# A pipelined attention stage on one core: the order of the work in a step, masks added by 32-row tiles, and one of eight sums of squares taken by ScalarE

## The reference, cut to what matters

```python
def attn_layer(x, Wqkv, qs, ksc, Wo):
    q, k, v = split(x @ Wqkv)             # 16 heads of 64
    q = l2norm(q) * qs; k = l2norm(k) * ksc
    q = q*cos*scale + rotate_half(q)*sin*scale
    k = k*cos/scale + rotate_half(k)*sin/scale
    # per window of 32 queries and 64 keys
    sim = where(mask, -max, 8.0 * q @ k.T)
    return concat_heads(softmax(sim) @ v) @ Wo
for i in range(6):
    x = attn_layer(shift_tokens(x), ...) + x
    x = ffn_layer(shift_tokens(x), ...) + x     # layernorm, gated gelu, 128 -> 341 -> 128
```

## Time and profile before

| What | Value |
|---|---|
| Median of 3 runs | 2125.77 us |
| Lowest and highest | 2125.34 and 2126.13 us |
| The profiled execution's own time | 2125.36 us |
| Its span, first to last instruction | 2123.6 us |
| Busy: PE, PEld, DVE, ACT, POOL | 1930.0, 1456.1, 1688.3, 1421.5, 1246.3 us |
| Mean granted TensorE clock, as a share of full speed | 0.955 |

### The profile page before, as it was taken

How to read it: one execution, slowest core, us unless ns; L and a number is a source line. 1 busy time by engine, 2 the same in 40 slices (tenths; PEclk the granted TensorE clock), 3 DMA queues, 4 the chain that set the end, 5 groups by cost and what they waited for, 6 DMA issues and landing times. The chain is left out here.

```text
span 2123.6 us, 79458 instructions
## 1 busy us (share of the span) xinstructions
PE 1930.0 (91%) x33524; PEld 1456.1 (69%) x33524; DVE 1688.3 (80%) x3905; ACT 1421.5 (67%) x5112; POOL 1246.3 (59%) x871
## 2 busy tenths in 40 slices
PE   5779999999999999999999999999999995494496
PEld 3358778687786886868868778687686872252374
DVE  5679889698796996978969889698796965795654
ACT  4269779597795985968959779597695972342121
POOL 2268768388584885857858668587584851031000
PEclk9879999999999999999999999999999998696798
DMA  3011122031120211212112121021120110001000
GB/s 114 0 46 42 29 53 57 20 79 34 45 59 22 75 42 36 57 31 72 42 25 63 40 54 54 20 67 48 41 55 18 42 34 13 0 2 61 1 1 21
DMA packets 88229, 85.72 MB, mean 40 GB/s; under 512 B 15392, under 2 KB 83008, under 8 KB 87232
## 3 DMA queue, kind: packets, MB, share of 16 engines
q1 hardware_dynamic: 87872, 80.63, 13.8%
HBM read 25.51 MB, written 1.05 MB: 13 GB/s over the span
## 5 line engine op out<-in xcount | busy, mean ns | idle before, releaser
L1082 POOL TENSOR_TENSOR RN<-N,minus_half 128x8 f32<-128x8 f32 x384 | 632.7, 1648 | 168.8 <-DVE N L1010 168.8
L920 ACT ACTIVATE PB<-PS,NMX 128x64 f32<-128x64 f32 x1536 | 471.4, 337 | 29.9 <-DVE NMX L1030 29.8
L679 PE MATMUL PS<-WQ,XS 128*128 128x256 f32 x1536 | 436.2, 407 | 7.4 <-SPq L623 6.5
L920 ACT ACTIVATION_READ_ACCUMULATOR PB<-PS,NMX 128x1 f32 x1536 | 348.0, 227 | 0.0
L679 PEld LDWEIGHTS PS<-WQ,XS 128*128 128x128 f32 x1536 | 262.3, 190 | 44.9 <-SPq L623 6.9
L1077 POOL TENSOR_TENSOR RR<-R 128x512 f32<-128x512 f32 x192 | 244.9, 1275 | 78.3 <-DVE QK L1040 78.3
L903 ACT ACTIVATE QKT<-PS 128x512 f32<-128x512 f32 x384 | 229.5, 598 | 84.8 <-PE PS L765 84.7
L1077 POOL TENSOR_TENSOR RR<-R1B,R2B 128x512 f32<-128x512 f32 x192 | 245.0, 1276 | 69.2 <-DVE QK L1040 69.2
L1040 DVE SCALAR_TENSOR_TENSOR QK<-RN,RR 128x512 f32<-128x512 f32 x384 | 261.8, 682 | 0.6 <-POOL RR L1077 0.6
L1010 DVE TENSOR_REDUCE N<-SQ 128x8 f32<-128x512 f32 x384 | 259.6, 676 | 0.0
L886 ACT ACTIVATE SQ<-PS 128x512 f32<-128x512 f32 x384 | 236.5, 616 | 9.4 <-PE PS L679 9.2
(11 more groups left out here) (270 smaller groups left out, 3516.9 us busy)
## 6 DMA issues: line engine op xcount, KB each, us to landing
VS<-XB SPq DMA_DIRECT2D x384, 96.0 KB, 2.1
VS<-XB SPq DMA_DIRECT2D x288, 32.0 KB, 2.1
WQ<-in_wqkv SPq DMA_DIRECT2D x40, 192.0 KB, 2.6
WO<-in_wo SPq DMA_DIRECT2D x6, 512.0 KB, 3.9
XS<-XT SPq DMA_DIRECT2D x10, 256.0 KB, 3.3
XS<-XT SPq DMA_DIRECT2D x10, 255.8 KB, 4.1
BIG<-in_wgu SPq DMA_DIRECT2D x1, 2048.0 KB, 8.0
W<-in_w SPq DMA_DIRECT2D x6, 341.0 KB, 3.3
```

Source lines behind the costliest of these rows:

```text
L679: mm = nc.tensor.matmul(PQ[:, m % 2, j * 256:(j + 1) * 256], XSb[b][:, t0:t0 + P], WQ[:, pair * 384:pair * 384 + 256], start=True, stop=True)
L920: ex = nc.scalar.activation(PB[:, g % 2, u, :], SC[:, h, DH * t:DH * t + DH], ACT.Exp, bias=NMX[:, u:u + 1], accum_out=PSUMS[:, g % 2, u:u ...
L1082: nc.gpsimd.tensor_tensor(RN[:, g % 2, :], N2[:, g % 2, :], minus_half[:, :], ALU.pow)
```

## The change

Three things change, all in stage B's step. One: the order. PE issues `project_qk(g + 3)` behind the transposes and the values rather than ahead of them; ACT issues the squares ahead of the copy `XB`; DVE issues the reciprocal behind `R2`, and `QK` (L1040) behind that, ahead of the scaling of the probabilities and the maxima. Two: the two mask matmuls of 128x128 become eight of 32x32 tiles on the diagonal, each with 128 columns of mask. Three: ACT's one square of 512 columns becomes one of 64 columns that also gives its sum into column 7 of `N2` (`accum_out`) and one of 448; DVE's sum reads 448 columns and writes seven sums. `N2` gets four buffers in place of two.

```diff
@@ -112,7 +112,7 @@
         XB = sb("XB", [P, CH, 512])
         VS = sb("VS", [P, CH, CB, P])
         SQ = sb("SQ", [P, 2, 8, DH])
-        N2 = sb("N2", [P, 2, 8])
+        N2 = sb("N2", [P, 4, 8])
         RN = sb("RN", [P, 2, 8])
         R1 = sb("R1", [P, CB, 256])
         R1B = sb("R1B", [P, CB, 256])
@@ -756,8 +756,6 @@
                     def step(g):
                         values, probs, ffn, tail = (there(g), there(g - 2), feed_forward_at(g),
                                                      feed_forward_at(g - 1))
-                        if there(g + 3) and not tail:
-                            project_qk(g + 3)
                         if there(g):
                             pe.wait_ge(qk_in.sem, qk_in.take())
                             for k in range(2):
@@ -788,6 +786,8 @@
                                                         start=True, stop=True)
                         if values or probs:
                             last.then_inc(vp_ps.sem, 1)
+                        if there(g + 3) and not tail:
+                            project_qk(g + 3)
                         if tail:
                             down(1)
                         if there(g):
@@ -795,10 +795,12 @@
                             if g > 0:
                                 pe.wait_ge(sc_free.sem, sc_free.take())
                             for h in range(2):
-                                nc.tensor.matmul(
-                                    SC[:, h, 0:P], identb[:, :],
-                                    bandmask[:, 0 if c == 0 else 1, :, :].rearrange("p t k -> p (t k)"),
-                                    start=True, stop=False)
+                                for w in range(4):
+                                    rows = slice(WIN * w, WIN * w + WIN)
+                                    nc.tensor.matmul(
+                                        SC[rows, h, 0:P], identb[rows, rows],
+                                        bandmask[rows, 0 if c == 0 else 1, :, :].rearrange("p t k -> p (t k)"),
+                                        start=True, stop=False)
                         if there(g):
                             c = g % CH
                             pe.wait_ge(qkt_in.sem, qkt_in.take())
@@ -883,8 +885,10 @@
 
                     def squares(m):
                         act.wait_ge(proj_in.sem, proj_in.take())
-                        nc.scalar.activation(SQ[:, m % 2, :, :].rearrange("p g d -> p (g d)"),
-                                             PQ[:, m % 2, :], ACT.Square).then_inc(sq_in.sem, 1)
+                        nc.scalar.activation(SQ[:, m % 2, 7, :], PQ[:, m % 2, 7 * DH:], ACT.Square,
+                                             accum_out=N2[:, m % 4, 7:8])
+                        nc.scalar.activation(SQ[:, m % 2, 0:7, :].rearrange("p g d -> p (g d)"),
+                                             PQ[:, m % 2, 0:7 * DH], ACT.Square).then_inc(sq_in.sem, 1)
 
                     def outputs(m):
                         l, b, pair, c = where(m)
@@ -905,13 +909,13 @@
                                 TQ.rearrange("p (k s) -> p k s", k=2), ACT.Copy).then_inc(qkt_in.sem, 1)
                         if there(g - 4) and not feed_forward_at(g - 1):
                             outputs(g - 4)
+                        if there(g + 3) and not feed_forward_at(g - 1):
+                            squares(g + 3)
                         if values or probs:
                             cols = slice(0 if values else 256, 512 if probs else 256)
                             act.wait_ge(vp_ps.sem, vp_ps.take())
                             nc.scalar.activation(XB[:, g % CH, cols], PX[:, cols], ACT.Copy)\
                                 .then_inc(vp_in.sem, 1)
-                        if there(g + 3) and not feed_forward_at(g - 1):
-                            squares(g + 3)
                         if there(g):
                             act.wait_ge(nmx_in.sem, nmx_in.take())
                             for h in range(2):
@@ -1007,18 +1011,24 @@
                                     dve.sem_inc(qks_free.sem, 1)
                             dve.wait_ge(sq_in.sem, sq_in.take())
                             nc.vector.tensor_tensor(R1k[g % 2][:, :, :], qk, COSk[l % 2][:, t, :], ALU.mult)
-                            nc.vector.tensor_reduce(N2[:, g % 2, :], SQ[:, g % 2, :, :], AX.X, ALU.add)\
+                            nc.vector.tensor_reduce(N2[:, (g + 2) % 4, 0:7], SQ[:, g % 2, 0:7, :], AX.X, ALU.add)\
                                 .then_inc(n2_in.sem, 1)
                         k = (g - 1) % 2
-                        if there(g - 1):
-                            dve.wait_ge(sc_free.sem, g)
-                            nc.vector.reciprocal(RO[:, k, :], PSUMS[:, k, :]).then_inc(ro_in.sem, 1)
                         if there(g + 2):
                             nc.vector.tensor_tensor(
                                 R2s[g % 2].rearrange("p j g v d -> p (j g) v d"),
                                 qk5[:, :, :, ::-1, :].rearrange("p j g v d -> p (j g) v d"),
                                 SINs[l % 2][:, t, :, :, :].rearrange("p j g v d -> p (j g) v d"), ALU.mult)\
                                 .then_inc(rot_in.sem, 1)
+                        if there(g - 1):
+                            dve.wait_ge(sc_free.sem, g)
+                            nc.vector.reciprocal(RO[:, k, :], PSUMS[:, k, :]).then_inc(ro_in.sem, 1)
+                        if there(g + 1):
+                            dve.wait_ge(rr_in.sem, rr_in.take())
+                            nc.vector.scalar_tensor_tensor(QKg[(g + 1) % 2], RN[:, (g + 1) % 2, :].unsqueeze(2)
+                                                           .to_broadcast([P, 8, DH]), 1e12, RRg,
+                                                           ALU.min, ALU.mult)\
+                                .then_inc(qk_in.sem, 1)
                         if there(g - 1):
                             dve.wait_ge(ro_in.sem, ro_in.take())
                             nc.vector.tensor_tensor(
@@ -1035,12 +1045,6 @@
                         tail = feed_forward_at(g - 1)
                         if there(g) and not tail:
                             maxima()
-                        if there(g + 1):
-                            dve.wait_ge(rr_in.sem, rr_in.take())
-                            nc.vector.scalar_tensor_tensor(QKg[(g + 1) % 2], RN[:, (g + 1) % 2, :].unsqueeze(2)
-                                                           .to_broadcast([P, 8, DH]), 1e12, RRg,
-                                                           ALU.min, ALU.mult)\
-                                .then_inc(qk_in.sem, 1)
                         if tail:
                             feed_forward(*tail)
                             if there(g):
@@ -1079,7 +1083,7 @@
                                 .then_inc(rr_in.sem, 1)
                         if there(g + 2):
                             pool.wait_ge(n2_in.sem, n2_in.take())
-                            nc.gpsimd.tensor_tensor(RN[:, g % 2, :], N2[:, g % 2, :], minus_half[:, :],
+                            nc.gpsimd.tensor_tensor(RN[:, g % 2, :], N2[:, (g + 2) % 4, :], minus_half[:, :],
                                                     ALU.pow)
                         if feed_forward_at(g - 1):
                             feed_forward(*feed_forward_at(g - 1))
```

## The result

The changed kernel takes 2151.05 us (median of 4, 2150.53 to 2153.58), the kernel before 2125.56 beside it (2125.30 to 2126.13): +25.5 us, ratio 1.0122, 95% interval 1.0104 to 1.0139. It is slower. The forecast was 2160, its own range 2148 to 2172.

The account below looks back on a forecast made before the run. PE's own queue was taken to set the 3.26 us step; +51.8 us for the mask tiles less 18.4 for the order gave +33.4, forecast 2160 us, own range 2148 to 2172, wider range 2120 to 2199.

Parts of the forecast that it names:

- the ring: Waits in the step from QK through transposes, QKT, scores and maxima to the next QK; closes in 3.25 us, below 3.26.
- The new order: On PE's queue, a cheaper exposed first weight load saves 0.05 us in 368 steps, 18.4 us in all.
- The mask tiles: On PE, eight 32*32 tiles for two full matmuls add 0.135 us a step, 51.8 us; bounds 0.025 and 0.36 more.
- my three parts: Mask cost on PE: form change ahead 0.09, eight tiles with the next change 0.25, less 0.205 us for matmuls removed.
- The eighth sum: On ACT, the accumulating square adds 0.10 to 0.24 us a step, hidden behind PE and costed at nothing.
- XB's ring: ACT's squares and XB wait for L679, PE's next step for XB; closes in 3.15 to 3.25 us, slack 0.1 to 0.2.
- B: On PE, the form change 32*32 to 64*32 is free: -9 us, 2117; chance 0.08.
- the sign that I had set for it: In PE's profile, L810 following the last mask matmul after 0.06 us and not 0.15 would show the free-change rival right.
- C: The ring of waits through QK and maxima sets the step, and opening it pays: -42 us, 2084; chance 0.04.
- D: The new wait on XB's path binds, making the step 3.45 us: 38 us above the forecast, 2199; chance 0.10.
- E: On PE, the eight mask tiles run one after another: 138 us above the forecast, 2298; chance 0.03.
- F: On PE, the form change ahead of the masks costs nothing: -1 us, 2125, no difference; chance 0.07.

Follow-up runs that it names:

- the doubled masks: Against the changed kernel, each of the eight 32*32 mask tiles is added twice; 2194.02 us, ratio 1.0318 to the kernel before.
- the scores' form: Against the changed kernel, the eight mask tiles are 64*32 like the scores; 2121.30 us, or 2122.99 us with the tiles in the scores' order.

## Why the prediction was right, step by step

**What bounds the kernel.** Right. The two edits that touch PE's queue change the time (-15 and +40 us), those that don't, don't (0 and 0). The sum of the parts, 40.4 - 15.1 = +25.3, is the +25.5 of the whole, so that within some 3 us for each part no interaction is left to explain. That the ring fits below the step was right too, but its working was not. L765 starts 0.34 us behind QK's end, not 0.13 (703.84 to 704.18), and the ring fits with about 0.2 us to spare (3.03 against 3.26), not with some hundredths. The forecast used neither figure, so nothing came of it.

**The new order.** I counted 0.05 us on 368 steps, -18.4. The order alone gave -15.1 (its interval reaches from -18 to -12, so that the forecast lies at its end), and the step went from 3.26 to 3.21. Right, including its source, the first load: four transposes at 0.66, L679 at 1.03.

**The mask tiles.** The mechanism was right, the size too large: +51.8 against +40.4 measured alone. Of my three parts, the change ahead of the masks (0.09) and what is removed (0.205) held. The mis-sized term is the block of eight tiles with its change, 0.25 us by the last eight of L826 and 0.22 measured. 0.03 x 384 = 11.5 us is the difference. Of these 0.03 us, 0.02 are what I added for a first load; the row of L826 itself gives 0.23. L826 was the nearest row but not the same: its loads have 64 columns and last 135 ns, those of the masks have 32 and last 89. That the shorter loads are the reason is argued from this; no run varied them. Bounds held: nothing was free, and nothing ran one after another.

**The change of form.** The Trainium skill (TensorEngine Tiling (Array Packing), Key Properties) says that a change of tiling mode, not of tile, drains the engine. The runs agree that the change of form is what costs; that the time is a drain they do not show. 32*32 to 64*32, which the trace before lacked, costs what the others cost, 0.09 us and a little load (0.11 by the doubled masks); with masks and scores in one form the scores begin after 0.07 us, and not 0.22.

**The eighth sum.** Costed at nothing, behind PE, and it is nothing (ratio 1.0000). The pair holds ACT 0.22 us, between my bounds of 0.17 and 0.31 and nearer to the lower one, where I had leaned to the upper.

**Waits.** XB's ring was forecast at 3.15 to 3.25 us, with 0.1 to 0.2 to spare; it closes in 3.10 or less. In the changed kernel XB ends at 704.61 and L776 starts at 704.96, 0.35 us later. I had the ring too long, on the safe side. DVE's idle time ahead of the maxima, forecast at 0.2 to 0.3 us: L1034 to L1040 takes 0.59, where L1040 to the next takes 0.34, so 0.25.

**Rivals.** B fails by the sign that I had set for it: the last mask matmul starts at 706.66 (706.59 + 0.29 less the 0.22 of one) and L812 follows 0.15 later, not 0.06. It fails again by the doubled masks and by the scores' form; C by the run without PE's edits; D by the one without masks; E by the doubled masks, 0.11 us for eight more tiles; F by the mask tiles alone, where the change ahead of them is seen. The step came to 3.32 for a forecast of 3.35, the total to 2151 for 2160: the masks' term was 11 us too high, and the order's gain, 3 us less than counted, takes part of that back.

## What to carry to other kernels

When an engine is full, look whether its instructions follow each other at the pitch of their own work; if they do, a cheaper order on the other engines gives nothing. A ring of waits is not measured by following it round once, for that always gives one step; add up its links without the time spent waiting. Count the changes of array form in a TensorE step as you count matmuls: here each that the traces separate costs some 0.09 us, four fifths of a float32 instruction of 128 columns (0.11), and small tiles that need a form of their own can cost more than the full matmul which they replace. Reorder on several engines together: the one move that gained 15 us would have cost 228 without its counterparts on VectorE and ScalarE.

## What the runs showed that I had not expected

Masks and scores in one form lose no time between them, yet the score instructions then take 0.46 us in place of 0.38, in either order of the tiles. The steps of the runs put a price on each way to add the masks: without them 3.10 us, with the two full matmuls 3.21, with eight tiles in the scores' form 3.24, with eight of 32*32 3.32. The full matmuls, which look the most wasteful, are the cheapest. And the order alone leaves two queues full at once, PE with 50.00 and DVE with 49.99 of 50 us; to take work off DVE then gives nothing, while to take work off PE as well does: without masks 24.5 us more, until ACT's queue is full too.
